# Three-stage decoder on one core: the slot stage's beat reordered, scores taken of unnormed slots, routing and last norm partly moved to GpSimd, mamba feeds issued one state earlier

## The chip, the cores and the metric

One core of a Trainium2 chip. The metric is the device time of one execution, in microseconds. Engines are named as in the profile: PE (TensorE), DVE (VectorE), ACT (ScalarE), POOL (GpSimd), SP (SyncE, which issues DMAs).

## The reference, cut to what matters

```python
x = layernorm(x + mamba(x))            # x is 64 x 128 x 128, float32; 16 states a channel
x = layernorm(x + slots(x, ctx_1024))  # each sequence's 128 tokens are its slots; 77 context rows
x = layernorm(x + experts(x))          # 8 experts, the one of the largest sigmoid(x @ Wr + br)

# mamba:   dt = softplus(dt_low @ W_dt + b_dt)
#          h = h * exp(A * dt_t) + (x_t * dt_t) * B_t ;  y = h . C_t            (a scan over time)
# slots:   Pn = rmsnorm(P) ; k = Pn @ Wk.T ; v = Pn @ Wv.T
#          three times:
#              sn = rmsnorm(slots) ; scores = (sn @ Wq.T) . k * SCALE
#              attn = softmax over slots ; attn = attn / (sum over context rows + 1e-6)
#              slots = gru_cell(attn . v, slots)
# experts: out = max(route) * (gelu(x @ W1[e]) @ W2[e]) with e = argmax(route)
```

The mamba's inner width is 256; its two halves are handled side by side.

## The kernel before

The program has three stages, one after the other on the core, each with its own list of instructions for every engine. Engines meet only through semaphores.

**Mamba stage** (lines 87 to 640). Sixteen groups g of four sequences, 512 columns each. Within a group the 16 states n follow each other. For a state ACT makes the decays (L395) and a copy of B (L401), DVE makes the input of the scan from the copy (`feed`, L492) and runs two scans (L503), POOL multiplies the state by C (`hc`, L323), PE adds it up (L606). For the four states n in `POOL_FEEDS = [3, 7, 11, 15]` POOL makes the scan's input instead (L311). While a group runs, pieces of the next group's preparation are put between the states by tables: `PE_SLOT`, `ACT_SLOT` (relu L361 and abs L363 of each half, exp L366, ln L369), `DVE_SLOT`, `POOL_SLOT` (dt L295, dtx L299). `over_groups` runs the groups, most of them in a hardware loop.

**Slot stage** (lines 643 to 1416). Two lanes of four sequences make a pair; eight pairs i follow each other (`over_pairs`: pairs 0, 1, then a hardware loop of three times two pairs, then 6 and 7). A pair has six beats, three iterations for each of two lanes. In a beat one lane (a) does its attention while the other (b) does its GRU (`beats`). The attention's chain is: sum of squares on PE (`ssq` L1336), `ms` on DVE (L1094), its root by a power on POOL (`rs` L912), its spread over partitions on PE (`root_spread` L1342), normed slots on DVE (`sn` L1098), scores on PE (L1348), maximum and its negative on DVE (L1102, L1104), four exponentials with their sums on ACT (L1007), reciprocal `rse` on DVE, denominators on PE (`den` L1354), `dn` and `rdn` on DVE (L1112, L1114), their spread on PE (`den_spread`, L1360, "dbc"), and the weights `at` on DVE (L1120). The GRU's chain begins with these weights: gates r, xn, z on PE (`gate_x` L1380), tanh `tr` on ACT, `rh`, `pre` on DVE, tanh `nn` and `tz` on ACT, `df`, `zd` and the new `h` on DVE.

Beside it runs the work on the next pair's context and on the last pair's result. The context's squares are ACT's (`sum_ctx`, L968), its norm is POOL's (`norm_ctx`, L904 and L908), the projections are named pieces in two places of each beat (`U_PLACE`): P transposes, K keys, v values, and for the pair before tp (tokens with the residual, L1324) and ct (counts for the routing). The last norm, choice of expert and place in the expert's list are small instructions on DVE; POOL scatters the rows by indirect DMA (`scatter`, L922).

```python
def hold(eng, sem, value, passed):
    eng.wait_ge(sem, value)
    eng.sem_inc(passed, 1)
```

`hold` is a wait that also counts itself. What stands behind a wait on an engine waits with it: each engine runs its list in order.

**Expert stage** (from line 1419): each expert's rows are loaded, computed and scattered back. The change leaves it alone.

## Time and profile before

| | us |
|---|---|
| three runs | 1895.29, 1900.54, 1902.24 (median 1900.54) |
| profiled execution | 1899.14, its span 1897.4 |
| PE busy / weight loads | 1542.0 (81%) / 913.9 |
| DVE busy | 1345.8 (71%) |
| POOL busy | 1096.0 (58%) |
| ACT busy | 1054.6 (56%) |
| mean granted TensorE clock | 0.916 of full |

The mamba stage fills the time to about 990 us, the slot stage that to about 1710, the expert stage the rest. Times of the views are us from the span's start. In a timeline a row's second number is its duration; in brackets stands how long the engine was idle before it and whose instruction ended that. Instructions of an engine overlap a little, so a start may come before the last one's end. Of a merged row ("x8") the duration is from the first's start to the last's end.

### The profile page before, as it was taken

To read this page: it belongs to the slowest core of one execution; us is meant where nothing else is said; L and a number is where in the kernel's file an instruction comes from. 1 tells how busy PE (TensorE), PEld (TensorE's weight loads), DVE (VectorE), ACT (ScalarE), POOL (GpSimd) and SP (SyncE) were. 2 spreads that over 40 slices of the span, in tenths; PEclk is the share of its full clock that TensorE was granted. 3 is DMA by queue.
4 is the path that set the end of the run, shared out by engine and by line. 5 is a ranking of instruction groups with operands and counts; after the bars stand their busy time and mean duration, and the time that the engine had idled before them with its cause. 6 is when DMAs were issued, how large, how long until landed. Compare 5 with 4: busy or idle time off the path is not lost. (4 is left out here: it accounts for less than half of the span.)

```text
span 1897.4 us, 24582 instructions
## 1 busy us (share of the span) xinstructions
PE 1542.0 (81%) x6146; PEld 913.9 (48%) x6146; DVE 1345.8 (71%) x2482; ACT 1054.6 (56%) x2119; POOL 1096.0 (58%) x649
## 2 busy tenths in 40 slices
PE   3898878988788887898765888888888888846995
PEld 1333323333233333333223666666666666735994
DVE  2999989989899798999961556666555666653543
ACT  3676766757677566776633545444444544322553
POOL 1889988889888798889961111422213141231666
PEclk8899989999899899999896999999899999867997
DMA  4354444444445354444415202122020200005772
GB/s 141 135 162 159 142 143 133 162 154 147 141 134 162 130 171 141 134 162 151 139 46 219 94 4 94 37 82 100 16 96 16 94 12 6 7 19 158 206 208 64
DMA packets 105884, 214.42 MB, mean 113 GB/s; under 512 B 12163, under 2 KB 56710, under 8 KB 105745
## 3 DMA queue, kind: packets, MB, share of 16 engines
q1 hardware_dynamic: 101200, 204.50, 32.8%
q0 software_dynamic: 4544, 8.47, 1.3%
q14 instruction: 102, 0.83, 0.1%
q8 instruction: 38, 0.62, 0.1%
HBM read 168.28 MB, written 45.56 MB: 113 GB/s over the span
## 5 line engine op out<-in xcount | busy, mean ns | idle before, releaser
L323 POOL TENSOR_TENSOR hc<-state,c_rows 128x1024 f32<-128x1024 f32 x256 | 599.5, 2357 | 101.4 <-DVE state L503 99.5
L503 DVE TENSOR_TENSOR_SCAN state<-ps_da,inp 128x512 f32<-128x512 f32 x512 | 591.7, 1206 | 56.2 <-POOL inp L311 56.2
L606 PE MATMUL ps_y<-hc,ident 128*128 128x512 f32 x1024 | 522.9, 647 | 114.8 <-POOL hc L323 114.7
L395 ACT ACTIVATE ps_da<-dt,a_neg 128x512 f32<-128x512 f32 x512 | 349.2, 688 | 195.9 <-DVE state L503 192.2
L606 PEld LDWEIGHTS ps_y<-hc,ident 128*128 128x128 f32 x1024 | 198.9, 203 | 418.2 <-issue 219.5
L492 DVE TENSOR_TENSOR inp<-dtx,ps_b 128x1024 f32<-128x1024 f32 x192 | 231.6, 1206 | 38.6 <-ACT ps_b L401 19.7
L912 POOL TENSOR_TENSOR rs<-ms,m_half 128x4 f32<-128x4 f32 x48 | 54.0, 1125 | 301.1 <-DVE ms L1094 301.1
L552 PE MATMUL ps_misc<-x1T,w_conv 128*128 (+4 forms) x256 | 128.9, 652 | 43.1 <-ACT x1T L346 34.9
L311 POOL TENSOR_TENSOR inp<-dtx,b_rows 128x1024 f32<-128x1024 f32 x64 | 150.6, 2353 | 0.0
L401 ACT COPY ps_b<-b_rows 128x512 f32<-128x512 f32 x192 | 111.2, 579 | 30.5 <-DVE inp L492 21.2
L1021 ACT ACTIVATE tr<-ps_r,bias 128x512 f32<-128x512 f32 x48 | 33.0, 687 | 149.2 <-PE ps_r L1380 149.2
L552 PEld LDWEIGHTS ps_misc<-x1T,w_conv 128*128 128x128 f32 x256 | 52.5, 211 | 117.4 <-issue 93.7
L1549 POOL DMA_INDIRECT out_x<-orow,target x78 | 77.5, 993 | 43.0 <-ACT orow L1568 23.5
L904 POOL TENSOR_TENSOR ctx_r<-ctx_ss,m_half 77x4 f32<-77x4 f32 x16 | 16.1, 1005 | 133.7 <-DVE ctx_ss L1090 133.6
L1578 ACT ACTIVATE act_h<-ps_h 128x512 f32<-128x512 f32 x78 | 46.6, 597 | 82.1 <-PE ps_h L1686 82.1
L922 POOL DMA_INDIRECT sorted_x<-row,dest x64 | 69.9, 1092 | 34.9 <-DVE dest L1216 17.6
L1007 ACT ACTIVATE ex<-ps_s,nmx 77x128 f32<-77x128 f32 x192 | 67.3, 360 | 24.1 <-DVE nmx L1104 23.9
L1695 PEld LDWEIGHTS ps_yy<-w,act_h 128*128 128x128 f32 x624 | 75.7, 192 | 1.9
L1348 PE MATMUL ps_s<-sn,kq 128*77 128x128 f32 x384 | 62.2, 315 | 17.1 <-DVE sn L1098 17.1
L1695 PE MATMUL ps_yy<-w,act_h 128*128 128x128 f32 x624 | 75.8, 275 | 0.0
L1026 ACT ACTIVATE nn<-pre,bih 128x512 f32<-128x512 f32 x48 | 34.7, 722 | 73.7 <-DVE pre L1128 73.7
L1125 DVE SCALAR_TENSOR_TENSOR rh<-tr,hnb 128x512 f32<-128x512 f32 x48 | 33.3, 694 | 59.6 <-ACT tr L1021 59.6
(207 smaller groups left out, 2721.7 us busy)
## 6 DMA issues: line engine op xcount, KB each, us to landing
b_rows<-bc_rows SPq DMA_DIRECT2D x128, 512.0 KB, 4.7
c_rows<-bc_rows SPq DMA_DIRECT2D x128, 512.0 KB, 3.9
sorted_x<-pad_rows SPq DMA_DIRECT2D x8, 4160.0 KB, 13.2
w<-in_L_ffn_W SPq DMA_DIRECT2D x78, 256.0 KB, 3.0
xrow<-sorted_x SPq DMA_DIRECT2D x39, 130.0 KB, 2.3
x_tok<-in_x SPq DMA_DIRECT2D x16, 256.0 KB, 3.4
ctx<-in_ctx SPq DMA_DIRECT2D x16, 154.0 KB
out_x<-orow,target POOLq DMA_INDIRECT x78, 2.9
```

Of the source, the lines that this page charges most:

```text
L311: pool.tensor_tensor(inp[:, n % RING], dtx[:, par], over_c(b_rows[:, slot, n % 2]), ALU.mult).then_inc(pool_fed, 1)
L323: pool.tensor_tensor(hc[:, n % RING], state[:, n % RING], over_c(c_rows[:, slot, n % 2]), ALU.mult).then_inc(hc_ready, 1)
L395: act.activation(ps_da[u % DA_RING][:], dt[:, par, c], ACT.Exp, scale=a_neg[:, c, n:n + 1]).then_inc(da_ready, 1)
L401: act.copy(ps_b[:], b_rows[:, slot, n % 2]).then_inc(b_copied, 1)
L492: dve.tensor_tensor(inp[:, n % RING], dtx[:, par], over_c(ps_b[:]), ALU.mult).then_inc(dve_fed, 1)
L503: dve.tensor_tensor_scan(state[:, n % RING, c], ps_da[u % DA_RING][:], inp[:, n % RING, c], 0.0, ALU.mult, ALU.add).then_inc(state_ready, 1)
L552: ins = pe.matmul(blocks[:, :, s:], w_conv[:, KW - 1 - s, c * P:(c + 1) * P], x_slot(g).rearrange("p (b l) -> p b l", l=P)[:, :, 0:P - s], ...
L606: ins = pe.matmul(ps_y[:, c], ident[:], hc[:, n % RING, c], start=False, stop=n == NS - 1)
L922: pool.indirect_dma_start(xs, bass.IndirectOffsetOnAxis(ap=dest[lane][:, b:b + 1], axis=0), row[lane][:, b, :], None).then_inc(scattered[l ...
L1007: act.activation(ex[lane][:, b * P:(b + 1) * P], ps_s[lane][0:M, b * P:(b + 1) * P], ACT.Exp, bias=nmx[lane][:, b:b + 1], accum_out=se[lan ...
L1549: pool.indirect_dma_start(out_rows, bass.IndirectOffsetOnAxis(ap=target[:, buf, s:s + 1], axis=0), orow[:, buf, s], None, bounds_check=NT ...
L1695: ins = pe.matmul(ps_yy[par][:, s * P:(s + 1) * P], act_h[:, par, c, s * P:(s + 1) * P], w2[:, buf, c], start=c == 0, stop=c == FC - 1)
```

## The change

In the mamba stage:

- POOL's feed of a state is issued four states ahead instead of three, behind the preparation pieces, also across the border of two groups.
- PE makes both halves of dt before state 8; ACT does relu and abs of both halves at state 9 in a row, exp and ln at state 10 instead of 11.

In the slot stage:

- `sn` is gone: scores are taken of the raw slots h. ACT copies them to SBUF (`sc`), DVE multiplies them by the root, which PE spreads into the bank `ps_hn`.
- Sum of squares and scores of the next beat's lane are done at the end of PE's beat, `ms` at the end of DVE's, the root `rs` at the end of POOL's.
- `ssq` and `den` are matmuls of one column (N=1). The 1e-6 comes in through an extra row of `ex` and `rse`, so `dn` is gone.
- The three matmuls of h (`gates_h`) are apart: hn and r before den, z between den and its spread.
- The order of the context pieces is new (`U_PLACE`); counts (ct0, ct1) are no longer pieces, but three matmuls into `ps_xn` (`count`), and VectorE adds its list's base to them straight from PSUM.
- POOL takes from DVE: residual, last norm's eps, rows and logits (`normed`), labels, the cast of the destinations, the context's mean.
- `scatter(0, i-1)` is done in beat 5, behind the context's norm and before the root of the next beat; `scatter(1, i-2)` in beat 0.
- Before the first beat: slots are loaded and squared ahead of the context pieces, the second context's DMA stands ahead of the DMAs of padding on SP.

```diff
...
-    PE_SLOT = {0: "xT", 1: "xb0", 2: "xb1", 6: "dbl", 8: "dt0", 9: "dt1"}
-    ACT_SLOT = {1: ["xT"], 3: ["xch0", "th0"], 4: ["xch1", "th1"], 7: ["dbl"], 9: ["relu0", "abs0"], 10: ["relu1", "abs1"],
-                11: ["exp", "ln"]}
+    PE_SLOT = {0: ["xT"], 1: ["xb0"], 2: ["xb1"], 6: ["dbl"], 8: ["dt0", "dt1"]}
+    ACT_SLOT = {1: ["xT"], 3: ["xch0", "th0"], 4: ["xch1", "th1"], 7: ["dbl"], 9: ["relu0", "abs0", "relu1", "abs1"],
+                10: ["exp", "ln"]}
...
-                if n + 3 in POOL_FEEDS:
-                    feed(g, par, n + 3)
                 if not last:
...
+                if n + RING in POOL_FEEDS:
+                    feed(g, par, n + RING)
+                elif n + RING - NS in POOL_FEEDS and not last:
+                    feed(g + 1, 1 - par, n + RING - NS)
...
-    U_PLACE = {(0, 0): ["tp0"], (0, 1): ["P0"], (1, 0): ["K0"], (1, 1): ["tp1"],
-               (2, 0): ["v00", "v01"], (2, 1): ["v02", "v03"], (3, 0): ["P1"], (3, 1): ["K1"],
-               (4, 0): ["ct0", "v10"], (4, 1): ["v11"], (5, 0): ["ct1"], (5, 1): ["v12", "v13"]}
...
+    U_PLACE = {(0, 0): ["P0"], (0, 1): ["tp0"], (1, 0): ["K0"], (1, 1): ["tp1"],
+               (2, 0): ["v00"], (2, 1): ["v01"], (3, 0): ["v02"], (3, 1): ["v03", "P1"],
+               (4, 0): ["K1"], (4, 1): ["v10", "v11"], (5, 0): ["v12"], (5, 1): ["v13"]}
...
-            pool.wait_ge(ctx_ms[k], q + 1)
-            pool.tensor_tensor(ctx_r[:, k], ctx_ss[:, k], m_half[0:M], ALU.pow).then_inc(ctx_root[k], 1)
-            pool.wait_ge(ctx_root[k], q + 1)
+            hold(pool, ctx_sumsq[k], q * GB + GB, passed2[1])
+            pool.tensor_scalar_add(ctx_r[:, k], ctx_ss[:, k], RMS_EPS).then_inc(ctx_root[k], 1)
+            hold(pool, ctx_root[k], 2 * q + 1, passed2[1])
+            pool.tensor_tensor(ctx_r[:, k], ctx_r[:, k], m_half[0:M], ALU.pow).then_inc(ctx_root[k], 1)
+            hold(pool, ctx_root[k], 2 * q + 2, passed2[1])
...
+        def residual(lane, q, par):
+            pool.wait_ge(dve2[lane], ev(V2, "h", q * ITERS + ITERS - 1))
...
+            pool.tensor_tensor(res2[lane][:], h[par][lane][:], x1T[:, bass.ds(g * T, T)], ALU.add).then_inc(post_p[lane], 1)
...
+        def normed(lane, q):
+            hold(pool, post_v[lane], ev(POSTV, "aggr", q), passed2[1])
+            pool.tensor_scalar_add(rstd2[lane][:], mv2[lane][:, :, 1], LN_EPS).then_inc(post_p[lane], 1)
+            hold(pool, post_p[lane], ev(POSTP, "veps", q), passed2[1])
+            pool.tensor_tensor(rstd2[lane][:], rstd2[lane][:], m_half[:], ALU.pow).then_inc(post_p[lane], 1)
...
+            hold(pool, scattered[lane], 16 * GB * q, passed2[1])
+            for b in range(GB):
+                ins = pool.tensor_scalar(row[lane][:, b, 0:P], tok[lane][:, b, 0:P], mv2[lane][:, b, 0:1], rstd2[lane][:, b:b + 1], ALU.subtract, ALU.mult)
...
+            pool.tensor_tensor(lg[lane][:], tok[lane][:, :, P:], over_e(rstd2[lane][:]), ALU.mult).then_inc(post_p[lane], 1)
...
+            pool.tensor_tensor(lg[lane][:], lg[lane][:], b_r[:].rearrange("p (o e) -> p o e", o=1).broadcast_to([P, GB, NE]), ALU.add).then_inc(post_p[lane], 1)
...
-            pool.wait_ge(post_v[lane], ev(POSTV, "dest", q))
+            hold(pool, post_v[lane], ev(POSTV, "dest_f", q), passed2[1])
+            pool.tensor_copy(dest[lane][:], dest_f[lane][:]).then_inc(post_p[lane], 1)
...
-            for beat, (a, it, j, q, _), _ in beats(i, par):
-                root(a, it)
-                if beat in (0, 1) and not first and not (isinstance(i, int) and i == 1):
-                    scatter(beat, i - 2)
+            for beat in range(2 * ITERS):
+                if beat in (0, 1) and not first:
+                    residual(beat, i - 1, 1 - par)
+                if beat == 0 and not first and not (isinstance(i, int) and i == 1):
+                    scatter(1, i - 2)
                 if beat in (1, 2) and not first:
-                    post_rooting(beat - 1, i - 1)
+                    normed(beat - 1, i - 1)
                 if beat == 2 and not last:
                     norm_ctx(i + 1, 1)
+                if beat in (3, 4) and not first:
+                    labels(beat - 3, i - 1)
                 if beat == 5 and not last and not (isinstance(i, int) and i == NQ - 2):
                     norm_ctx(i + 2, 0)
+                if beat == 5 and not first:
+                    scatter(0, i - 1)
+                after_this = following(beat, i, par, last)
+                if after_this is not None:
+                    root(*after_this[:2])
...
-                attention_sq(a, it, j, q, par)
...
+                attention_exp(a, it)
                 for name in u_names(beat, 0, first, last):
                     read_u(i, par, name)
-                attention_exp(a, it)
+                after_this = following(beat, i, par, last)
+                if after_this is not None:
+                    attention_sq(*after_this)
                 gru_h(a, it)
                 for name in u_names(beat, 1, first, last):
                     read_u(i, par, name)
+                if after_this is not None:
+                    attention_scores(*after_this[:2])
...
+        def maxima(lane, it):
+            dve.wait_ge(scored[lane], it + 1)
             dve.wait_ge(pe1[lane], ev(PE1, "rbc", it))
...
+            dve.tensor_tensor(sc[lane][:], sc[lane][:], ps_hn[0:M], ALU.mult).then_inc(dve1[lane], 1)
+            hold(dve, dve1[lane], ev(V, "s", it), passed2[0])
...
                 if working:
-                    gate_n(b, it2)
-                slots_normed(a, it, par)
+                    reset(b, it2)
+                    new_in(b, it2)
+                maxima(a, it)
                 if working:
                     update(b, it2, par2)
-                maxima(a, it)
-                if working:
                     new_h(b, it2, par2)
+                normaliser(a, it)
                 if beat in (1, 2) and not first:
                     statistics(beat - 1, i - 1)
-                if beat in (3, 4) and not first:
-                    highest(beat - 3, i - 1)
...
-                if beat in (3, 4) and not first:
-                    first_highest(beat - 3, i - 1)
-                denominators(a, it)
                 if beat in (4, 5) and not first:
                     ranks(beat - 4, i - 1)
                 if beat in (3, 4) and not first:
+                    highest(beat - 3, i - 1)
+                denominators(a, it)
+                weights(a, it)
+                if beat in (4, 5) and not first:
+                    destinations(beat - 4, i - 1)
+                if beat in (3, 4) and not first:
                     chosen_expert(beat - 3, i - 1)
...
+                after_this = following(beat, i, par, last)
+                if after_this is not None:
+                    mean_sq(*after_this[:2])
...
+                    pe.wait_ge(post_v[1], ev(POSTV, "base", i - 2))
...
-                scores(a, it, par)
+                if beat in (4, 5) and not first:
+                    count(beat - 4, i - 1, b, it2)
                 for name in u_names(beat, 0, first, last):
                     make_u(i, par, name, first, last)
-                gates_h(a, it, j, q, par)
+                gate_h(a, it, par, "hn", other, it2)
+                gate_h(a, it, par, "r", other, it2)
+                den(a, it)
                 for name in u_names(beat, 1, first, last):
                     make_u(i, par, name, first, last)
-                den(a, it)
+                gate_h(a, it, par, "z", other, it2)
                 den_spread(a, it)
+                after_this = following(beat, i, par, last)
+                if after_this is not None:
+                    c, it3, j3, q3, par3 = after_this
+                    if beat == 5:
+                        pe.wait_ge(u_read, u_value(i, "v13"))
+                    ssq(c, it3, a, it)
+                    scores(c, it3, par3)
...
```

### Where instructions stand

POOL in the mamba stage, first group, at states 10 to 15: hc is the state times C, inp the feed of a state by POOL, dt and dtx the next group's preparation. Before:

```order
L323 TENSOR_TENSOR hc<-state,c_rows 128x1024 [waits c_loaded1,y_added,state_ready]
L295 TENSOR_TENSOR dt<-relu,softp 128x1024 [waits act_pre]
L323 TENSOR_TENSOR hc<-state,c_rows 128x1024 [waits c_loaded1,y_added,state_ready]
L299 TENSOR_TENSOR dtx<-dt,xb 128x1024 [waits dve_pre,pool_pre]
L303 MEMSET dt 128x8 [waits pool_pre]
L323 TENSOR_TENSOR hc<-state,c_rows 128x1024 [waits c_loaded2,y_added,state_ready]
L311 TENSOR_TENSOR inp<-dtx,b_rows 128x1024 [waits state_ready,b_loaded3]
L323 TENSOR_TENSOR hc<-state,c_rows 128x1024 [waits c_loaded2,y_added,state_ready]
L323 TENSOR_TENSOR hc<-state,c_rows 128x1024 [waits c_loaded3,y_added,state_ready] x2
```

The change:

```order
L324 TENSOR_TENSOR hc<-state,c_rows 128x1024 [waits c_loaded1,y_added,state_ready]
L295 TENSOR_TENSOR dt<-relu,softp 128x1024 [waits act_pre]
L324 TENSOR_TENSOR hc<-state,c_rows 128x1024 [waits c_loaded1,y_added,state_ready]
L299 TENSOR_TENSOR dtx<-dt,xb 128x1024 [waits dve_pre,pool_pre]
L303 MEMSET dt 128x8 [waits pool_pre]
L311 TENSOR_TENSOR inp<-dtx,b_rows 128x1024 [waits state_ready,b_loaded3]
L324 TENSOR_TENSOR hc<-state,c_rows 128x1024 [waits c_loaded2,y_added,state_ready] x2
L324 TENSOR_TENSOR hc<-state,c_rows 128x1024 [waits c_loaded3,y_added,state_ready] x2
```

The feed that waits for `b_loaded3` (states 7 and 15) stood between the two hc of `c_loaded2`; behind dtx it now stands ahead of both, and the feed for `b_loaded1` of the next group (its state 3) closes the group.

ACT at states 9 to 11 of the same group: relu L361 (L364) and abs L363 (L366) write relu and softp, L366 and L369 (L369 and L372) are exp and ln, ps_b is the copy of B, ps_da a decay. Before:

```order
L401 COPY ps_b<-b_rows 128x512 [waits dve_fed,b_loaded1]
L395 ACTIVATE ps_da<-dt,a_neg 128x512 [waits state_ready] x3
L361 ACTIVATE relu<-ps_misc,b_dt 128x512 [waits pool_pre,misc_full]
L363 ACTIVATE softp<-ps_misc,b_dt 128x512
L395 ACTIVATE ps_da<-dt,a_neg 128x512 [waits state_ready]
L401 COPY ps_b<-b_rows 128x512 [waits dve_fed,b_loaded2]
L395 ACTIVATE ps_da<-dt,a_neg 128x512 [waits state_ready]
L361 ACTIVATE relu<-ps_misc,b_dt 128x512 [waits pool_pre,misc_full]
L363 ACTIVATE softp<-ps_misc,b_dt 128x512
L395 ACTIVATE ps_da<-dt,a_neg 128x512 [waits state_ready]
L401 COPY ps_b<-b_rows 128x512 [waits dve_fed,b_loaded2]
L395 ACTIVATE ps_da<-dt,a_neg 128x512 [waits state_ready]
L366 ACTIVATE softp<-softp 128x1024 [waits act_pre]
```

The change:

```order
L404 COPY ps_b<-b_rows 128x512 [waits dve_fed,b_loaded1]
L398 ACTIVATE ps_da<-dt,a_neg 128x512 [waits state_ready] x3
L364 ACTIVATE relu<-ps_misc,b_dt 128x512 [waits pool_pre,misc_full]
L366 ACTIVATE softp<-ps_misc,b_dt 128x512
L364 ACTIVATE relu<-ps_misc,b_dt 128x512 [waits pool_pre,misc_full]
L366 ACTIVATE softp<-ps_misc,b_dt 128x512
L398 ACTIVATE ps_da<-dt,a_neg 128x512 [waits state_ready]
L404 COPY ps_b<-b_rows 128x512 [waits dve_fed,b_loaded2]
L398 ACTIVATE ps_da<-dt,a_neg 128x512 [waits state_ready]
L369 ACTIVATE softp<-softp 128x1024 [waits act_pre]
```

Both relu/abs pairs now stand ahead of the first decay and copy, and exp one copy and two decays earlier.

POOL at the end of pair 1 of the slot stage: ctx_r and pn are the norm of the context of the pair after next, rs is the root of the slots. Before:

```order
L904 TENSOR_TENSOR ctx_r<-ctx_ss,m_half 77x4 [waits ctx_ms0]
L908 TENSOR_TENSOR pn<-ctx,ctx_r 77x512 [waits u_full,ctx_root0]
L820 UNCONDITIONAL_BRANCH
L820 ISA
L912 TENSOR_TENSOR rs<-ms,m_half 128x4 [waits dve1_0]
L919 ISA
L40 ISA [waits post_v0]
L922 DMA sorted_x<-row,dest 67584x130 [waits padded]
L922 DMA sorted_x<-row,dest 67584x130 x3
L912 TENSOR_TENSOR rs<-ms,m_half 128x4 [waits dve1_1]
```

The change:

```order
L914 TENSOR_SCALAR ctx_r<-ctx_ss 77x4 [waits ctx_sumsq0]
L916 TENSOR_TENSOR ctx_r<-ctx_r,m_half 77x4 [waits ctx_root0]
L920 TENSOR_TENSOR pn<-ctx,ctx_r 77x512 [waits ctx_root0,u_full]
L959 CAST dest<-dest_f 128x4 [waits post_v0]
L963 DMA sorted_x<-row,dest 67584x130 [waits padded,post_p0]
L963 DMA sorted_x<-row,dest 67584x130 x3
L924 TENSOR_TENSOR rs<-ms,m_half 128x4 [waits dve1_0]
L818 UNCONDITIONAL_BRANCH
L818 ISA
```

The scatter of lane 0 stood behind the next beat's root; now it stands ahead of it, behind the context's norm, which has one instruction more.

## Rows read from the trace of the kernel before

**Rows 1.** Windows: us, then busy time (x instructions) of PE, PEld, DVE, ACT, POOL

```profile
9.00:984.00 975.00, 813.51 (x1720) 327.35 (x1721) 861.92 (x811) 655.55 (x1022) 820.50 (x368) 0.92 0.44 143
...
1040.00:1600.00 560.00, 476.49 (x2876) 370.88 (x2877) 333.32 (x1047) 266.46 (x783) 130.54 (x119) 0.96 0.14 55
```

**Rows 2.** VectorE's waits: instruction, releaser, us in total, times, longest

```profile
DVE state L503 <- POOL inp L311: 56.2, 15, 3.8
```

**Rows 3.** Timeline of POOL: start us, duration, engine, line, out<-in, [idle before <-releaser]

```profile
254.81 2.35 POOL L295 TENSOR_TENSOR dt<-relu,softp 128x1024 f32<-128x1024 f32 x1 [1.35 <-ACT softp L369]
...
261.93 0.11 POOL L303 MEMSET dt<- 128x8 f32 x1 [0.15 <-POOL dtx L299]
...
264.49 2.34 POOL L311 TENSOR_TENSOR inp<-dtx,b_rows 128x1024 f32<-128x1024 f32 x1
```

**Rows 4.** Timeline of DVE, the scan of state 15, same group

```profile
266.95 1.22 DVE L503 TENSOR_TENSOR_SCAN state<-ps_da,inp 128x512 f32<-128x512 f32 x1 [3.74 <-POOL inp L311]
```

**Rows 5.** Timeline of ACT between the stages

```profile
1013.73 0.31 ACT L968 ACTIVATE ctx_sq<-ctx 77x128 f32<-77x128 f32 x1 [7.86 <-DMA ctx<-in_ctx]
...
1035.62 0.36 ACT L1007 ACTIVATE ex<-ps_s,nmx 77x128 f32<-77x128 f32 x1 [7.49 <-DVE nmx L1104]
```

**Rows 6.** The instructions of line 1112: durations in ns, first and last start

```profile
L1112 DVE TENSOR_SCALAR dn<-ps_s x48: 161/163/164, 1039.9 to 1675.3; 128x4 f32<-128x4 f32 x48
```

**Rows 7.** Timeline of ACT in the scan stage, a copy and one relu/abs pair

```profile
248.57 0.58 ACT L401 COPY ps_b<-b_rows 128x512 f32<-128x512 f32 x1
...
249.70 0.68 ACT L361 ACTIVATE relu<-ps_misc,b_dt 128x512 f32<-128x512 f32 x1
```

**Rows 8.** Timeline of one beat of the slot stage

```profile
1613.44 1.12 DVE L1120 SCALAR_TENSOR_TENSOR at<-ex,rse,ps_s 77x128 f32<-77x128 f32 x4 [0.76 <-PE ps_s L1360]
...
1617.26 0.69 DVE L1128 TENSOR_TENSOR pre<-rh,ps_xn 128x512 f32<-128x512 f32 x1
...
1617.86 0.68 DVE L1098 TENSOR_TENSOR sn<-h,ps_s 128x512 f32<-128x512 f32 x1
...
1621.06 0.36 ACT L1007 ACTIVATE ex<-ps_s,nmx 77x128 f32<-77x128 f32 x1 [1.78 <-DVE nmx L1104]
...
1623.49 1.16 PE L1354 MATMUL ps_s<-rse,ex 77*128 77x128 f32 x8 [0.30 <-DVE rse L1108]
...
1625.12 0.66 PE L1360 MATMUL ps_s<-ident,rdn 128*77 128x128 f32 x4 [0.47 <-DVE rdn L1114]
```

**Rows 9.** Timeline of PE: context work within beats

```profile
1216.90 1.45 PE L1318 MATMUL ps_u<-vw_w,pnT 128*77 128x384 f32 x4
...
1622.11 1.09 PE L1324 MATMUL ps_u<-w_rows,res 128*128 128x136 f32 x8
```

**Rows 10.** Timeline of a late root, and the new-gate matmul (hn) before and after

```profile
1218.19 1.02 PE L1369 MATMUL ps_hn<-h,whhT 128*128 128x512 f32 x2
...
1228.09 1.21 POOL L908 TENSOR_TENSOR pn<-ctx,ctx_r 77x512 f32<-77x512 f32 x1 [0.16 <-POOL ctx_r L904]
...
1229.27 1.00 POOL L912 TENSOR_TENSOR rs<-ms,m_half 128x4 f32<-128x4 f32 x1
...
1231.01 0.69 DVE L1098 TENSOR_TENSOR sn<-h,ps_s 128x512 f32<-128x512 f32 x1 [1.79 <-PE ps_s L1342]
...
1233.89 1.80 PE L1369 MATMUL ps_hn<-h,whhT 128*128 128x512 f32 x2
```

**Rows 11.** Timeline of POOL: first and last DMA of one scatter

```profile
1190.13 1.19 POOL L922 DMA_INDIRECT sorted_x<-row,dest  x1 [0.20 <-issue]
...
1194.44 0.99 POOL L922 DMA_INDIRECT sorted_x<-row,dest  x1 [0.30 <-issue]
```

**Rows 12.** Timeline of POOL: the last pair's first scatter DMA

```profile
1700.25 1.03 POOL L922 DMA_INDIRECT sorted_x<-row,dest  x1 [9.79 <-DVE dest L1216]
```

**Rows 13.** Timeline: residual on DVE, root on POOL

```profile
1602.69 0.68 DVE L1145 TENSOR_TENSOR res<-h,x1T 128x512 f32<-128x512 f32 x1
...
1602.84 1.39 POOL L912 TENSOR_TENSOR rs<-ms,m_half 128x4 f32<-128x4 f32 x1 [11.62 <-DVE ms L1094]
```

310 lines of the change are left out of this document (140 added, 170 removed).

## The prediction

> **What bounds the kernel now.** I read the busy time by stage first. In the scan stage (9 to 984 us) VectorE works 861.9 of 975 us and GpSimd 820.5: it is bound by work, near the edge. In the slot stage (1040 to 1600 us) TensorE works 476.5 of 560 and VectorE 333.3: no engine is full, so there the chain from instruction to instruction sets the time [rows 1]. The expert stage is not touched.
>
> Next I read the waits. VectorE's costliest one in the scan stage is for GpSimd's last feed: 56.2 us in 15 waits, one in each group that prepares a next one [rows 2]. The timeline says why: GpSimd starts dt at 254.81, after 1.35 of idle time, and reaches the feed of state 15 only at 264.49, with two hc and dtx in between [rows 3]; the scan of state 15 waits 3.74 for it [rows 4]. A group lasts 57.5, and 22 GpSimd instructions of about 2.35 fill 51.5 of it: GpSimd has 6 us to spare, so the wait is one of order, not of work.
>
> Between the stages ScalarE waits 7.86 us for the second context's DMA, and the first exponential starts at 1035.62 [rows 5]. In the slot stage I count beats by the "dn" instruction, one a beat: 48 from 1039.9 to 1675.3, so 47 intervals in 635.4 us, 13.5 each [rows 6].
>
> **The change part by part.**
>
> *Feeds four ahead, dt earlier.* The feed of state 15 moves ahead of the hc of state 12. By the same durations it starts at 254.8 - 1.0 + hc + hc + dtx = about 260.3 and ends at 262.65; its scan can start at 264.2 at the earliest, so the 3.74 goes. What is late next: ScalarE now runs both relu/abs pairs in one piece. Each pair takes 1.2, and the copy of B for state 12, at 248.57 [rows 7], then ends 1.1 later, at 250.3, where VectorE wants it at 249.4: 0.9 lost, and about 0.4 at the next feed. So 1.3 is given back in each group: 56.2 - 15 x 1.3 = **-36.7 us**. Bounds: -56 (ScalarE catches up unseen) and 0 (the same work, bunched, or a feed that now waits for the scan whose buffer it takes, gives all back). Those 1.3 come from the rows before and after, which I replayed, so I take that value.
>
> *Prologue.* The loads and squares of the slots come before the context's reads, and the second context's DMA before the pad DMAs on SP's queue. After: the slot squares, root and raw scores lie beside the context work, and the first exponential comes when root and spread are there, at about 1023.2 instead of 1035.6: **-12.4** (bounds -15 and -5, should the second context's DMA still hold ScalarE).
>
> *A plain beat.* Count from the end of the weights ("at", 1613.44 + 1.12 = 1614.56). "pre" begins 2.70 later [rows 8]. In the change TensorE ends its beat with the next lane's sums and scores, 1.1 of scores, so the first gate begins about 0.3 later: pre at 3.0. Behind it VectorE multiplies the copied scores by the root (3.6; sn followed pre by 0.60), maximum 4.35, nmx 5.05, exponentials 5.25 to 6.75; meanwhile df, zd and h fill VectorE to 7.2, where the reciprocal goes; then den 7.4, reciprocal straight from PSUM 8.6 (den to spread took 1.63 with one more small instruction, now gone), the spread behind the z gate 9.25, "at" 9.95 to 11.05 [rows 8]. The normed slots (0.68), and scores after them (1.1 on TensorE), are what the chain loses. Plain beats of 11.1 stand against the 13.5 that beats of all kinds take now, though the context work and the late roots below come on top.
>
> *Context work* in TensorE's second place stands between den and the spread and adds in full: token projections 1.0 each (of 1.09), 14 times; a v 0.65 (two took 1.45) [rows 9]; P1, four narrow transposes, I estimate at 0.45 from these. By the new table beats 0 and 1 hold a projection, beats 2, 3, 4 and 5 hold v01, v03 and P1, v10 and v11, and v13: 14 + 7 x (0.65 + 1.1 + 1.35 + 0.65) = **+40 us**.
>
> *Roots that come late.* The root is now last in GpSimd's beat, behind the context norm. From "rs" (1229.27 + 1.00) to VectorE's use went 0.74 [rows 10]; since VectorE wants it at 3.6, a root that ends more than 2.9 after "at" delays the beat by the excess. In beat 3 of 7 pairs the context's squares follow the copy of the scores on ScalarE and end at 2.85; then the small add, a power of 1.0, pn 1.21, rs 1.00 [rows 10] end at about 6.8: +3.9. TensorE, idle so long, drops: after such a wait hn took 1.80, where 1.02 is usual [rows 10], and scores lose as much: +1.8. Beat 0 of pair 1: the same. In beat 0 of pairs 2 to 6 the scatter's four DMAs stand between pn and rs as well: 1190.13 to 1195.43, 5.3 us [rows 11]. The root ends at about 13: +10.1 + 2.2 for the clock. Together 8 x 5.7 + 5 x 12.3 = **+107 us**. This is the term that eats the shorter beat; the bounds are 0 (if the scatter and norm find their inputs early) and +125.
>
> Sum of the stage: 47 x 11.1 + 40 + 107 = 669 against 635.4: **+33.5**.
>
> *Residual, rows, labels on GpSimd.* In the plain order they end before the root is due: I cost them at nothing. Their cover is GpSimd's own idle time: it works only 130.5 of 560 us [rows 1]. If the last norm, between the statistics (about 8.9 in its beat) and the root, takes over 5 us, the cover is gone (rival C).
>
> *Tail.* The first scatter DMA of the last pair starts at 1700.25 [rows 12]; fewer handovers on VectorE and counts in one step make it about 3 earlier: **-3** (bounds -6, +3).
>
> Sum: 1899.1 - 36.7 - 12.4 + 33.5 - 3 = 1880.5, say **1881 us**. The profiled execution (1899.14, span 1897.4) lies 1.4 below the median of the runs, 1900.5; I make no correction.
>
> *A rule against it.* A GpSimd root that started 0.15 after VectorE's residual began took 1.39 instead of 1.00, and ended 0.5 after it [rows 13]. The Trainium skill (SBUF — State Buffer, Who interferes with whom) says that a VectorE instruction with two SBUF inputs and a GpSimd instruction that reads SBUF take turns, whoever comes first holding the port for its whole instruction. This trace agrees as far as those rows go.
>
> **The rivals.**
>
> *B: the gains come undisturbed.* ScalarE hides the bunching (-19 against my sum: 1861), or in the late beats TensorE keeps 2.4 GHz and the roots come 1 or 2 us earlier (-25: 1856); both: 1836. For it: my replay has every instruction at its worst place. Against: 1.80 for hn is in the trace. Chance 0.22.
>
> *C, slower than before: the small GpSimd instructions.* On GpSimd a power of 4 columns takes 1.00 [rows 10], a memset of 8 columns 0.11 [rows 3]. The last norm is now add, power, four row scalings, a product and a sum on GpSimd. If each costs near 1 us, it takes 8 instead of some 4.5, and from 5 on it delays the root: 3 us in beat 2 and again in beat 3 of 7 pairs = +42, with +3 for the add and cast in the late ones: 1926. For it: the only small arithmetic in the trace costs 1.0. Against: a power is no add, pn over 512 columns takes 1.21. Chance 0.14.
>
> *D: the scan stage gains nothing.* The feed arrives, but the bunched relu/abs, or a feed now waiting for its buffer, costs VectorE 3.7 a group: 1881 + 37 = 1918. For it: VectorE has only 3.7 idle in 57.5, so any new wait shows. Chance 0.12.
>
> *E: the residuals and rows on GpSimd block VectorE.* Twice 1.2 us in each of 7 pairs on the chain is 17 at most; I take 10: 1891. It is the mechanism of [rows 13], and it is what the Trainium skill's port rule (same page and section) would make of this change. Chance 0.07.
>
> **How the numbers follow.** Forecast 0.45, B 0.22, C 0.14, D 0.12, E 0.07. The forecast's own range is 1866 to 1896. The range 1846 to 1918 takes in D, E and most of B, and leaves out C and B's both-at-once. Within 0.5%, about what a measurement of this kernel can tell from no change, is 1891 to 1910. Faster: 0.36 of the forecast + 0.22 of B = 0.58. Slower: 0.12 of C + 0.08 of D + 0.02 = 0.22. The rest, 0.20, is the same.
>
> **What would show it.** In the profile of the changed kernel: VectorE's wait of 3.7 before the scan of state 15 is gone and waits for the copy of B of about 0.9 and 0.4 stand in its place (D: they add up to 3.7 a group). First exponential near 1023 less the scan's gain. Beats between "at" rows: about 11.1 plain; about 17 in beat 3; 23 in beat 0 from pair 2 on, with VectorE waiting for the root's spread and the DMAs ahead of "rs" on GpSimd. The forecast is wrong if these long beats aren't there, or if beats 2 are long too, with the last norm on GpSimd over 5 us (C). Rows of VectorE's rh, df or zd over 1.2 us beside GpSimd work would be E.

## The result, and the profile after

The changed kernel takes 1930.19 us (median of 4 runs, 1927.03 to 1932.26) against 1899.18; the ratio is 1.0163, 95% interval 1.0138 to 1.0188. It is 31 us slower, where 18 us faster was forecast, and lies outside the stated range (1846 to 1918). The profiled execution took 1930.98, its span 1929.0, with a mean granted TensorE clock of 0.882 against 0.916.

Where the 31 us are can be read from the first and the last of the 48 beats. In what follows an interval is named by the beat in which it ends. In the changed kernel the reciprocal `rdn` (L1162) stands in the place of `dn`; [rows 6] is the row of before that answers to it.

```profile
L1162 DVE RECIPROCAL rdn<-ps_s x48: 148/182/183, 991.6 to 1704.8; 128x4 f32<-128x4 f32 x48
```

- Up to the first beat: 991.6 against 1039.9, **-48**. Forecast: -49.
- The 47 intervals between beats: 713.2 us against 635.4, **+78**. Forecast: +33.5.
- From the last beat to the end of the span: 224.2 against 222.1, **+2**. Forecast: -3.

The beginning came out as computed, the tail 5 us off; the bulk of the miss is the slot stage. The windows say how it changed (columns as in [rows 1]; the last three numbers of a row are the granted clock, the share of the DMA engines and GB/s):

```profile
9.00:984.00 975.00, 815.77 (x1784) 339.87 (x1784) 864.82 (x821) 674.05 (x1071) 829.93 (x394) 0.92 0.45 149
1040.00:1600.00 560.00, 441.61 (x2589) 337.94 (x2589) 257.96 (x747) 255.66 (x722) 194.03 (x264) 0.86 0.13 48
1672.00:1690.00 18.00, 18.00 (x69) 14.82 (x68) 7.42 (x24) 5.54 (x15) 1.59 (x4) 0.50 0.00 0
```

In the slot stage TensorE is busy for 441.6 of 560 us where it was 476.5 of 560, VectorE for 258 instead of 333, and the granted clock is 0.86 instead of 0.96. Only GpSimd got fuller, 194 against 130.5, and is far from full; the others wait more. VectorE's waits name for what (instruction, releaser, us in total, times, longest):

```profile
DVE rh L1173 <- ACT tr L1076: 117.5, 48, 5.7
DVE at L1168 <- PE ps_s L1358: 111.6, 48, 3.8
DVE sc L1150 <- PE ps_hn L1340: 79.8, 20, 9.8
...
DVE inp L495 <- ACT ps_b L404: 39.6, 38, 4.3
```

The wait of [rows 2] is gone altogether. In its place 19.9 us more stand in waits for the copy of B (19.7 before), 1.3 for each of 15 groups, as forecast. The three others are of the slot stage: the new gates, the weights behind the denominators' spread (all 48 times, 2.3 us each), and the scores behind the root's spread.

**The late root**, beat 0 of pair 2 (timeline; the weights of the beat before end at 1153.88):

```profile
1152.76 1.12 DVE L1168 SCALAR_TENSOR_TENSOR at<-ex,rse,ps_s 77x128 f32<-77x128 f32 x4 [1.83 <-PE ps_s L1358]
...
1154.96 0.31 ACT L1022 ACTIVATE ctx_sq<-ctx 77x128 f32<-77x128 f32 x1
...
1156.86 0.22 POOL L914 TENSOR_SCALAR ctx_r<-ctx_ss 77x4 f32<-77x4 f32 x1 [12.67 <-ACT ctx_sq L1022]
...
1157.27 1.59 POOL L916 TENSOR_TENSOR ctx_r<-ctx_r,m_half 77x4 f32<-77x4 f32 x1 [0.18 <-POOL ctx_r L914]
1157.27 0.69 DVE L1173 SCALAR_TENSOR_TENSOR rh<-tr,hnb 128x512 f32<-128x512 f32 x1 [2.87 <-ACT tr L1076]
...
1159.03 1.03 POOL L920 TENSOR_TENSOR pn<-ctx,ctx_r 77x512 f32<-77x512 f32 x1 [0.18 <-POOL ctx_r L916]
...
1161.20 1.24 POOL L963 DMA_INDIRECT sorted_x<-row,dest  x1 [1.00 <-POOL dest L959]
...
1165.27 0.96 POOL L963 DMA_INDIRECT sorted_x<-row,dest  x1 [0.30 <-issue]
...
1166.25 1.04 POOL L924 TENSOR_TENSOR rs<-ms,m_half 128x4 f32<-128x4 f32 x1
...
1168.53 0.68 DVE L1150 TENSOR_TENSOR sc<-sc,ps_hn 77x512 f32<-77x512 f32 x1 [9.75 <-PE ps_hn L1340]
...
1170.50 2.00 PE L1366 MATMUL ps_hn<-h,whhT 128*128 128x512 f32 x2
```

The context's squares follow the copy of the scores, then norm, cast, four DMAs, and only then the root. It ends at 1167.29, 13.4 us after the weights; 13 was forecast. One part of it has a cause of its own: the context's power began together with VectorE's rh and took 1.59 instead of 1.04 (more on this under rival E). VectorE waited 9.75 for the spread, and the hn matmul behind it took 2.00 instead of 1.02: 1.2 GHz. These five beats last 23.2 to 25.0 us (forecast 24), beat 3 of seven pairs 17.5 to 19.1 (forecast 17.4).

**A beat without a late root** (timeline; the weights of the beat before end at 1634.22):

```profile
1630.59 1.17 PE L1318 MATMUL ps_u<-w_rows,res 128*128 128x136 f32 x8
...
1631.60 1.02 PE L1370 MATMUL ps_z<-h,whhT 128*128 128x512 f32 x2
...
1634.62 1.06 PE L1379 MATMUL ps_r<-at,vw 77*128 77x128 f32 x8
...
1637.26 0.69 DVE L1178 TENSOR_TENSOR pre<-rh,ps_xn 128x512 f32<-128x512 f32 x1
...
1637.87 0.68 DVE L1150 TENSOR_TENSOR sc<-sc,ps_hn 77x512 f32<-77x512 f32 x1
...
1639.61 0.40 ACT L1062 ACTIVATE ex<-sc,nmx 77x128 f32<-77x128 f32 x1 [0.32 <-DVE nmx L1154]
...
1641.83 1.05 PE L1352 MATMUL ps_s<-rse,ex 78*128 78x1 f32 x8 [1.25 <-DVE rse L1158]
...
1642.75 2.16 PE L1318 MATMUL ps_u<-w_rows,res 128*128 128x136 f32 x8
...
1644.70 1.76 PE L1370 MATMUL ps_z<-h,whhT 128*128 128x512 f32 x2
```

The gate starts 0.40 after the weights, pre 3.04 (forecast 3.0), the scaled scores 3.65 (3.6), the exponentials 5.39 (5.25), den 7.61 (7.4): the replay holds to 0.2 us. But before den TensorE idles for 1.25 us, and the token projection and the z matmul behind it, 1.17 and 1.02 in the beat before, take 2.16 and 1.76; from 1643 to 1647 the granted clock is 0.60. So it is in beat 1 of four of seven pairs. This is not a late root; it is what the sum did not have. Over the whole stage, z took more than 1.4 us behind 9 of the 16 waits of 1.25 or 1.26, and behind none of the 15 waits of 0.57 to 0.77. That is an association: the beats with the shorter wait also hold more work ahead of it.

**The last norm on GpSimd**, same stretch:

```profile
1657.00 0.23 POOL L938 TENSOR_SCALAR rstd<-mv 128x4 f32<-128x4 f32 x1 [7.22 <-DVE mv L1198]
1657.41 1.04 POOL L940 TENSOR_TENSOR rstd<-rstd,m_half 128x4 f32<-128x4 f32 x1 [0.18 <-POOL rstd L938]
1658.76 3.13 POOL L944 TENSOR_SCALAR row<-tok,mv,rstd 128x128 f32<-128x128 f32 x4 [0.31 <-POOL rstd L940]
1661.86 0.24 POOL L946 TENSOR_TENSOR lg<-tok,rstd 128x32 f32<-128x32 f32 x1
1662.27 0.25 POOL L948 TENSOR_TENSOR lg<-lg,b_r 128x32 f32<-128x32 f32 x1 [0.18 <-POOL lg L946]
1662.48 1.03 POOL L924 TENSOR_TENSOR rs<-ms,m_half 128x4 f32<-128x4 f32 x1
```

Small instructions take 0.23 to 0.25, the power 1.04, but each row scaling 0.78: in all 5.5 us from the first start to the last end, just over the point of 5 at which the prediction's rival C begins. In pair 2, at 2.4 GHz, the weights ended at 1192.90 and the root behind such a norm at 1196.90: 4.0 us, where 2.9 was the limit. TensorE waits 1.71 for that root in beat 2 of pairs 2, 3 and 5; in the other pairs the root is there by 1.8.

In the tail both lanes' last norms stand on GpSimd one behind the other, 1715.4 to 1726.4. The last pair's first scatter begins at 1731.07, 26.3 us after the last beat, where it was 24.9 before [rows 12].

**The last pair.** Its beats 4 and 5 take 17.5 and 17.9 us, nearly all of it at 1.2 GHz (the third window above: 18 of 18 us busy, clock 0.50; it is 0.50 from 1690 to 1703, too). Eight small matmuls of a gate take 1.91 there, 1.06 elsewhere:

```profile
1694.53 1.91 PE L1379 MATMUL ps_xn<-at,vw 77*128 77x128 f32 x8
...
1699.93 2.05 PE L1366 MATMUL ps_hn<-h,whhT 128*128 128x512 f32 x2
```

### The profile page after: what moved, and what is told of

The parts are those of the page before. It is cut to its first block and busy times, and to the rows that moved or that the text cites. A ratio compares the mean times of both kernels' runs of the same rounds, so it can differ in the third digit from the quotient of the medians.

```text
span 1929.0 us, 24814 instructions
## 1 busy us (share of the span) xinstructions
PE 1559.3 (81%) x6178; PEld 937.2 (49%) x6178; DVE 1288.4 (67%) x2194; ACT 1083.0 (56%) x2151; POOL 1191.2 (62%) x863
## 5 line engine op out<-in xcount | busy, mean ns | idle before, releaser
L609 PE MATMUL ps_y<-hc,ident 128*128 128x512 f32 x1024 | 510.7, 641 | 98.2 <-POOL hc L324 98.0
L555 PE MATMUL ps_misc<-x1T,w_conv 128*128 (+4 forms) x256 | 123.5, 629 | 38.2 <-ACT x1T L349 29.9
L924 POOL TENSOR_TENSOR rs<-ms,m_half 128x4 f32<-128x4 f32 x48 | 49.3, 1028 | 160.2 <-DVE ms L1145 160.1
L1168 DVE SCALAR_TENSOR_TENSOR at<-ex,rse,ps_s 77x128 f32<-77x128 f32 x192 | 53.7, 339 | 111.6 <-PE ps_s L1358 111.6
L1340 PE MATMUL ps_hn<-ident,rs 128*77 128x128 f32 x192 | 37.9, 330 | 97.5 <-POOL rs L924 97.5
L1057 ACT COPY sc<-ps_s 77x512 f32<-77x512 f32 x48 | 27.9, 581 | 142.9 <-PE ps_s L1346 142.9
L1150 DVE TENSOR_TENSOR sc<-sc,ps_hn 77x512 f32<-77x512 f32 x48 | 32.6, 679 | 79.8 <-PE ps_hn L1340 79.8
L1352 PEld LDWEIGHTS ps_s<-rse,ex 78*128 78x128 f32 x384 | 51.8, 204 | 67.4 <-DVE rse L1158 58.4
L1080 ACT ACTIVATE tz<-ps_z,bias 128x512 f32<-128x512 f32 x48 | 32.4, 675 | 92.6 <-PE ps_z L1379 91.6
L1062 ACT ACTIVATE ex<-sc,nmx 77x128 f32<-77x128 f32 x192 | 74.5, 390 | 9.9 <-DVE nmx L1154 9.4
## 6 DMA issues: line engine op xcount, KB each, us to landing
sorted_x<-pad_rows SPq DMA_DIRECT2D x8, 4160.0 KB, 12.7
```

Of the source, the lines that this page charges most:

```text
L555: ins = pe.matmul(blocks[:, :, s:], w_conv[:, KW - 1 - s, c * P:(c + 1) * P], x_slot(g).rearrange("p (b l) -> p b l", l=P)[:, :, 0:P - s], ...
L609: ins = pe.matmul(ps_y[:, c], ident[:], hc[:, n % RING, c], start=False, stop=n == NS - 1)
L1062: act.activation(ex[lane][0:M, b * P:(b + 1) * P], sc[lane][:, b * P:(b + 1) * P], ACT.Exp, bias=nmx[lane][:, b:b + 1], accum_out=se[lane] ...
L1168: ins = dve.scalar_tensor_tensor(at[lane][:, s], ex[lane][0:M, s], rse[lane][0:M, b:b + 1], ps_s[lane][0:M, s], ALU.mult, ALU.mult)
```

## The experiments

Times are medians with the ratio to the kernel before on the same chip. The kernel before took 1899 to 1904 us on the chips used, so between runs of different chips the ratios are the better comparison. "Slot stage" is from first to last beat of the profiled execution.

**The scan stage alone**

```diff
 # m_all: kernel before, mamba stage of the change
 # m_feed: the same, but
-    PE_SLOT  = {... 8: ["dt0", "dt1"]}
-    ACT_SLOT = {... 9: ["relu0", "abs0", "relu1", "abs1"], 10: ["exp", "ln"]}
+    PE_SLOT  = {... 8: ["dt0"], 9: ["dt1"]}
+    ACT_SLOT = {... 9: ["relu0", "abs0"], 10: ["relu1", "abs1"], 11: ["exp", "ln"]}
```

> Edit: the kernel before with the change's mamba part alone (feeds four ahead, relu/abs of both halves in a row, exp and ln one state earlier); slot stage as before. Theory (the prediction's step on the scan stage holds): the 3.74 us before each scan of state 15 is gone and about 1.3 us a group of waiting for the copy of B comes in its place, so -37 us, about 1862, and the first dn of the slot stage at about 1002 instead of 1039.9. Rival (the gain in the changed kernel's scan stage came with its new prologue, or is given back behind it): less than 15 us gained, 1885 or more.

Measured: 1862.09, ratio 0.979 (0.9764 to 0.9815). The first beat starts at 1000.8, 39 us earlier than before, and its slot stage takes 633.7. So the scan stage's step stands, and of the changed kernel's -48 the prologue has 9.

> Edit: as m_all, but PE_SLOT and ACT_SLOT as before; only the order of GpSimd's feeds is the change's. Theory (bunching both relu/abs pairs is what makes the copies of B late): no new wait for the copy, and the feed of state 15, which now follows dt, hc and dtx from 254.8, ends at about 264.5, 0.3 us late: about 3.4 us gained in each of 15 groups, -51 us, about 1848. Rival (the waits for the copy come from feeding four ahead, not from the bunching): the same as m_all, about 1862.

Measured: 1868.56, ratio 0.9824 (0.9789 to 0.9858). Neither. The waits for the copy are gone as the theory says (14.2 us in all), but the scan of state 15 waits again:

```profile
DVE state L506 <- POOL inp L311: 20.0, 15, 1.5
```

1.3 us a group, where I had computed 0.3: with VectorE's 3.7 us gone the group is shorter, so the same ln comes later in it. GpSimd's waits for ln grew from 52.8 to 72.1 us in all. What a later step frees shortens the time an earlier one has. So bunching is not a loss here: with it (m_all) the first beat comes at 1000.8, without it at 1006.0.

**GpSimd's and ScalarE's order in the slot stage**

```diff
 # p_scatter: POOL, beat 5
+                if beat == 5 and not first:
+                    scatter(0, i - 1)
                 if beat == 5 and not last and ...:
                     norm_ctx(i + 2, 0)
-                if beat == 5 and not first:
-                    scatter(0, i - 1)
 # p_root: scatter(0), then root of the next lane, then norm_ctx (beats 2 and 5)
 # p_early: as p_root, and on ACT
+                    sum_ctx(...)                        # beats 2 and 5
                 if after_this is not None:
                     attention_scores(*after_this[:2])
-                    sum_ctx(...)
```

> Edit: the changed kernel with scatter(0, i-1) ahead of norm_ctx(i+2, 0) in GpSimd's beat 5. Theory (late roots make the long beats): the four DMAs then run while GpSimd would wait for the context's squares, so the root of beat 0 in pairs 2 to 6 ends 5 to 6 us earlier; these five beats fall from 23 to 25 us to about 18, the length of beat 3: -30 us, about 1900. Rival (the beats are long because TensorE runs at 1.2 GHz there, whatever comes late): the five beats keep over 22 us, less than 10 us gained.

Measured: 1901.11, ratio 0.999 (0.9971 to 1.0008), 29 below the changed kernel (33 by the ratios). The five beats take 18.4 to 18.8 us: the theory.

> Edit: the changed kernel with the next lane's root ahead of norm_ctx and of scatter(0) on GpSimd. Theory (late roots): beat 3 of 7 pairs falls from 18 to about 13.5 us (the context's squares on ScalarE still delay tr by 1.3); in beat 0 the root is in time, but residual(0) now stands behind norm and scatter and TensorE waits some 3 us for it: 17 to 18 us instead of 23 to 25. Together -60 to -70 us, 1860 to 1870. Rival (the clock alone): less than 20 us gained, with 1.2 GHz still in beats 0 and 3.

The text names the order wrongly: in the kernel scatter(0) stands ahead of the root, and only norm_ctx behind it. Measured: 1865.72, ratio 0.9798 (0.977 to 0.9827). Beat 3 takes 12.9 to 16.6 us, beat 0 13.9 to 16.9.

> Edit: the changed kernel with scatter(0) first, then the next lane's root, then norm_ctx on GpSimd, and with sum_ctx (the context's squares) ahead of the copy of the scores on ScalarE. Theory (late roots, and ScalarE's squares in front of tr): ScalarE idles about 2 us before that copy, so the 1.7 us of squares fit there; beat 3 falls to about 13.3 and beat 0 to about 13 us, against 18 to 25 in the changed kernel: 7 x 5 + 6 x 10 us = -95 us, about 1835. Rival (what is won on GpSimd is lost to pn coming late for P0 and P1, or to a TensorE at 1.2 GHz): not better than 1862.

Measured: 1840.29, ratio 0.9657 (0.9638 to 0.9676). Slot stage 627.8 us:

```profile
L1162 DVE RECIPROCAL rdn<-ps_s x48: 149/182/183, 991.2 to 1619.0; 128x4 f32<-128x4 f32 x48
```

Three steps of order alone, no instruction fewer, bring 90 us. It is the late roots that they take away: beat 0 of pairs 1 to 6 and beat 3 of pairs 0 to 6 take 268 us together in the changed kernel and 173 in p_early. The prediction put 107 on late roots.

**Work for TensorE in the last pair**

```diff
 # a_fill: changed kernel; f_fill: p_early
+                if last:
+                    filler(beat, place, i)   # beats 2 to 5: matmuls of K's and v's shape into ps_u, unread
```

> Edit: the changed kernel with matmuls in the last pair's beats 2 to 5, of the shapes and at the places that other pairs have for the context's K and v, their results unused. Theory (in the last pair TensorE has no context work, falls to 1.2 GHz in beats 4 and 5, and these take 17.5 and 17.9 us instead of 12.5): with the extra work they take 12 to 13 us, and the time falls by 8 to 11 us in spite of 8 more matmuls, to about 1920. Rival (the two beats are long for another reason, the counts for one): unchanged or up by 3 us, and still 17 us in both beats.

Measured: 1922.81, ratio 1.01 (1.0083 to 1.0117), 7 us less than without (12 by the ratios). The last two beats take 13.7 and 12.1 us; the granted clock is 0.88 from 1668 to 1682 and 1.00 from 1682 to 1694.

> Edit: p_early with the extra matmuls of a_fill. Theory (the two effects are independent): 8 to 11 us below p_early, about 1825. Rival (the low clock of the last pair is a matter of where the beats before it leave TensorE, and is gone with the late roots): the same as p_early within 3 us, or up by the extra work.

Measured: 1836.16, ratio 0.9639 (0.9623 to 0.9655), 4 less than p_early. The last two beats fell from 17.4 and 17.9 to 13.7 and 12.1; in the profiled execution of f_fill some others were long instead. The intervals of the two ratios touch, so here it is the two beats that show the effect, not the total. In a_fill work that nobody reads made the whole kernel faster: the clock was what made these beats long, not the counts.

**The last norm behind the root**

```diff
 # g_normed: f_fill, POOL
-                if beat in (1, 2) and not first:
-                    normed(beat - 1, i - 1)
                 ...
                     norm_ctx(i + 2, 0)
+                if beat in (1, 2) and not first:
+                    normed(beat - 1, i - 1)
```

> Edit: f_fill with normed (the last norm on GpSimd) behind the next lane's root and behind norm_ctx instead of ahead of them, in beats 1 and 2. Theory (normed takes 5.5 us on GpSimd, four row scalings of 0.78 the most of it, and so holds the root of beats 2 and 3 up by about 0.85 us, the point that the prediction put at 5 us for its rival C): beats 2 and 3 get 0.8 to 1 us shorter in 7 pairs, -11 to -14 us, about 1824. Rival (the root has slack there, and the beats are as long as they are through context work): within 3 us of f_fill's 1836.

Measured: 1837.69, ratio 0.966 (0.9643 to 0.9678), where f_fill has 0.9639: nothing gained, the rival. In f_fill the roots of beats 2 and 3 were in time already (TensorE waits for none of them; in pairs 1 to 7 they end 1.8 to 2.7 us after the weights), so there was nothing to gain. Beat 2 falls from 14.0 to 12.4 us in one pair and takes 13.8 or 13.9 in the six others. Rows of TensorE from one of these show why it is still long:

```profile
1241.89 1.05 PE L1362 MATMUL ps_s<-rse,ex 78*128 78x1 f32 x8 [1.26 <-DVE rse L1158]
1242.80 1.77 PE L1318 MATMUL ps_u<-w_rows,res 128*128 128x136 f32 x8
1244.37 1.91 PE L1380 MATMUL ps_z<-h,whhT 128*128 128x512 f32 x2
```

1.26 idle before den, then a projection of 1.77 and a z matmul of 1.91: half a microsecond and more each over their usual 1.17 and 1.02. In this run z took more than 1.4 us behind 21 of the 27 waits of 1.24 to 1.56, and behind none of the 14 waits of 0.57 to 0.66.

**The place of z's matmul**

```diff
 # g_z: g_normed; a_z: changed kernel. PE:
                 gate_h(a, it, par, "r", other, it2)
+                gate_h(a, it, par, "z", other, it2)
                 den(a, it)
                 for name in u_names(beat, 1, first, last):
                     make_u(i, par, name, first, last)
-                gate_h(a, it, par, "z", other, it2)
                 den_spread(a, it)
```

> Edit: g_normed with the h part of gate z ahead of den instead of between den and its spread. Theory (the chain decides: that matmul of 1.02 us stands between the denominators and their spread and only 0.3 of it is hidden): 0.7 us less in each of 47 beats, -33 us against g_normed, about 1791. Rival (TensorE's own work decides: about 10.6 us a beat without context work, so what leaves one place is paid in another, as den then starts later): less than 12 us gained, or even some lost where context work precedes hn.

Measured: 1771.64 (1761.90 to 1791.91), ratio 0.9291 (0.9257 to 0.9326): 66 us less than g_normed, twice what the theory gave. z fills the time before den, and in this beat the clock stays at its upper level:

```profile
1218.34 1.02 PE L1380 MATMUL ps_z<-h,whhT 128*128 128x512 f32 x2
1219.81 1.05 PE L1362 MATMUL ps_s<-rse,ex 78*128 78x1 f32 x8 [0.45 <-DVE rse L1158]
1220.72 0.85 PE L1312 MATMUL ps_u<-vw_w,pnT 128*77 128x384 f32 x2
```

Slot stage 553.6 us, 41 of 47 intervals of 10.7 to 11.9. Over 1040 to 1500 us the clock is 0.96 with TensorE busy for 436 of 460:

```profile
L1162 DVE RECIPROCAL rdn<-ps_s x48: 148/182/183, 993.1 to 1546.7; 128x4 f32<-128x4 f32 x48
...
1040.00:1500.00 460.00, 436.19 (x2747) 337.61 (x2747) 279.76 (x797) 272.35 (x764) 212.90 (x281) 0.96 0.16 58
```

and in g_normed 0.92 with 414:

```profile
1040.00:1500.00 460.00, 413.65 (x2454) 310.50 (x2454) 250.85 (x720) 247.96 (x698) 188.14 (x248) 0.92 0.15 57
```

The slot stage fell by 69 us from g_normed to g_z. At the 0.9 us a beat that the next run shows for the place alone it would have been 42; the rest, some 27 by this estimate, is the clock.

> Edit: the changed kernel with the h part of gate z ahead of den, as in g_z, and nothing else. Theory (two separate costs: z between den and its spread is 0.7 to 1 us in every beat, late roots are on top of it): 47 beats by 0.7 to 1 us, -33 to -47 us, about 1890; beats 0 and 3 stay long (17 to 24 us). Rival (g_z gained 66 us because TensorE, with the late roots gone, stayed at 2.4 GHz once its work was dense, and the place of z as such is worth little): with the late roots still there less than 20 us is gained.

Measured: 1901.67, ratio 0.9989 (0.9974 to 1.0004), 29 us less than the changed kernel (33 by the ratios, the theory's lower edge). Most beats without a late root take 11.0 to 11.9 us instead of 11.9 to 12.8, the 0.7 to 1 us of the theory; but beat 2 takes 15.7 to 15.9 in five pairs, where the changed kernel has 13.3 to 14.0, and gives part of it back. The cause stands in TensorE's rows:

```profile
1185.65 1.14 PE L1340 MATMUL ps_hn<-ident,rs 128*77 128x128 f32 x4 [2.14 <-POOL rs L924]
1186.59 1.91 PE L1379 MATMUL ps_z<-at,vw 77*128 77x128 f32 x8
```

In beat 2 of all seven pairs the root now stands 4.4 us after the weights, behind the last norm on GpSimd, TensorE waits 2.1 for it, and what follows mostly runs at 1.2 GHz. g_z, where that norm stands behind the root, has 11.2 to 11.5 there. So g_z has its gain from two things together: z ahead of den, and the norm out of the root's way.

**The scan stage once more**

```diff
 # g_mid: g_z with
-    PE_SLOT  = {... 8: ["dt0", "dt1"]}
-    ACT_SLOT = {... 9: ["relu0", "abs0", "relu1", "abs1"], 10: ["exp", "ln"]}
+    PE_SLOT  = {... 7: ["dt0"], 8: ["dt1"]}
+    ACT_SLOT = {... 8: ["relu0", "abs0"], 9: ["relu1", "abs1"], 10: ["exp", "ln"]}
```

> Edit: g_z with relu/abs of the two halves at states 8 and 9 instead of both at 9 (PE makes them before states 7 and 8), exp and ln at 10 as in the change. Theory (bunching makes the copies of B late, as m_all showed by 1.3 us a group, and m_feed lost as much by a later ln): the waits for the copy go and the feed of state 15 stays in time, so 15 to 20 us less in the scan stage than g_z. Rival (at state 8 ScalarE has less room than at 10, and the waits only move): within 5 us of g_z's scan stage.

Measured: 1751.27 (1744.87 to 1768.82), ratio 0.9194 (0.9165 to 0.9223). The waits for the copy are back at before's level,

```profile
DVE inp L495 <- ACT ps_b L404: 20.6, 8, 3.9
```

no scan waits for a feed, and the first beat starts at 976.3 instead of 993.1: 17 us. The whole is 20 us less than g_z (18 by the ratios). The profiled execution is the slowest of the four, and its slot stage took 566.7, so the 17 us are the surer figure. This is the fastest version of the study, 8% below the kernel before.

## Why the prediction was wrong

**Feeds four ahead, -36.7: right**, -39 in m_all, with the give-back of 1.3 us a group in the place that was named. Rival D (nothing gained) is refuted. The feed starts 7.3 us after dt (255.03 after 247.77), where the sum had 6.5; the scan did not need it sooner.

**Prologue, -12.4: right in kind, 9.2 measured** (1000.8 in m_all, 991.6 in the changed kernel).

**Roots that come late, +107: right.** The roots end 13.4 and 7.2 us after the weights (forecast 13 and 6.8), and the 13 intervals take 268 us, where the sum gives them 260. The prediction's mechanism for the whole is this one, and moving calls alone gave 90 us back.

**A plain beat, 11.1 in all 47 intervals: here it failed.** The chain was replayed well, at 2.4 GHz. What I left out is that a change that shortens TensorE's work and leaves it waiting changes the clock outside the late beats, too. I had put 1.8 to 2.2 us of low clock on each late beat and none on the others. The slot stage has 44 us more than the sum, and the five intervals that the sum has at 11.1 with nothing added took 12.1, 16.0, 12.7, 17.5 and 17.9:
- The last pair, 17 us over the sum: no late root, but also no context work from beat 2 on; 13 of it in two beats at 1.2 GHz. a_fill and f_fill show that it is the clock.
- Pair 0, 6 us: its second interval took 16.0 instead of 11.1, at 1.2 GHz.
- Pairs 1 to 6, 21 us together. Nearly 9 of it is in the interval that holds tp1, 12.1 in the sum. It takes 13.7 to 14.0 in pairs 1, 4 and 6 (and 7), in which the projection and z behind the wait before den run at 1.2 GHz, and 13.3 in pairs 2, 3 and 5, in which they don't and the norm on GpSimd holds the root up by 1.1. Another 7 is in beats 3, and 4 in beats 1.

The size of the hole shows best with the roots in time: the sum without its late roots is 562 us, and g_normed's slot stage took 622.4.

**Context work and z between den and its spread.** The prediction counted both in its 11.1 and +40, correctly, but as a fact of the change and not as its weakest point. z's place alone is 0.9 us a beat, and with z ahead of den more of the stage runs at 2.4 GHz (0.96 against 0.92). That the wait before den is what lets the clock fall is the likely reading, not a shown one: in g_z the clock also fell in beat 4 of two pairs, behind a wait of only 0.59. With all of it repaired the new beat takes 553.6 us for 47 intervals against 635.4 before: the idea of the change is good, its order is not.

**Residual, rows, labels on GpSimd, at nothing: too low, though by little here.** Rival C's mechanism (small instructions of 1 us each) is refuted, 0.23 to 0.25 each; but the row scalings, which it did not single out, take 0.78 each and bring the norm to 5.5 us. Its sign came in part: beats 2 are long, but only in three pairs because of the root. In a_z, with the shorter beat, the same norm holds up the root in all seven. That the measured time is near C's 1926 is chance.

**Tail, -3: wrong in sign, +2.** The last norms, moved to GpSimd, stand in the way there.

**Rival E, the port: its mechanism is real, its price was in other rows.** The prediction's sign for it, rh over 1.2 us beside GpSimd work, came once in the changed kernel:

```profile
1623.24 1.28 POOL L931 TENSOR_TENSOR res<-h,x1T 128x512 f32<-128x512 f32 x1
1623.82 1.25 DVE L1173 SCALAR_TENSOR_TENSOR rh<-tr,hnb 128x512 f32<-128x512 f32 x1 [1.70 <-ACT tr L1076]
...
1635.41 1.27 POOL L931 TENSOR_TENSOR res<-h,x1T 128x512 f32<-128x512 f32 x1
1636.44 0.79 DVE L1173 SCALAR_TENSOR_TENSOR rh<-tr,hnb 128x512 f32<-128x512 f32 x1 [2.15 <-ACT tr L1076]
```

Both rh end 0.55 after the residual's end, and so do the six others of 0.75 to 0.79; they are short only because they began 0.2 us before that end. By the rule of the Trainium skill (SBUF — State Buffer, Who interferes with whom) these two take turns for whole instructions, and these rows agree. On VectorE it costs little: rh takes 0.716 us on average where it took 0.694, 1 us over 48 beats. On GpSimd it costs more: the context's power, which begins with rh, takes 1.59 instead of 1.04 in 11 of the 13 late roots and 1.28 in another, 6 us in the chain of these beats. It is part of their 13.4 and 7.2. In g_z the overlap is worse, and rh takes 1.6 us in two intervals of 12.3:

```profile
1202.03 1.27 POOL L931 TENSOR_TENSOR res<-h,x1T 128x512 f32<-128x512 f32 x1
1202.24 1.61 DVE L1173 SCALAR_TENSOR_TENSOR rh<-tr,hnb 128x512 f32<-128x512 f32 x1 [2.15 <-ACT tr L1076]
```

The prediction read [rows 13] wrongly in one point: that root ended 0.86 after the residual, not 0.5.

**Rival B** (the gains undisturbed): neither half of it came. The copies of B wait 1.3 us a group, and the clock got worse, not better. It is also where the numbers went astray: by putting a chance on a kinder clock and none on a worse one, the range left out the side on which the result lies.

Still open: why in g_z and g_mid two beats 4 of 17.4 us remain, and some others of 14.3 to 16.7. In g_z the clock falls at 1233.5 with TensorE full and the DMA engines at their fullest (398 GB/s). The DMAs alone are not the reason: at 401 to 413 GB/s in pairs 1, 2 and 4 (1092 to 1100, 1160 to 1168, 1308 to 1316) the clock is 1.00.

## What to carry to other kernels

When a stage is bound by a chain, write down for each beat what each engine does while it waits, TensorE first: a matmul that can stand in the wait costs nothing there, costs most of its length behind it (0.9 of 1.02 us here), and its absence may cost the clock of what follows. Work that is last in one engine's beat and first in the next one's chain belongs ahead of everything that has slack, DMAs and squares above all. And when a change shortens an engine's work, price its clock again for every beat, not for those alone that get longer. Work moved to GpSimd has to be placed against VectorE's instructions in time: where the two take turns, whichever comes second pays.
